# An eight-block transformer kernel, one core: another hand-held order of work for the opening

## The chip, the cores and the metric

The kernel runs on one core of a Trainium2 chip. The metric is the device time of one execution in microseconds; the median of three runs stands for the kernel. Matrix products run on TensorE (PE), reductions and elementwise work on VectorE (DVE), activations and copies on ScalarE (ACT), more elementwise work on GpSimd (POOL), and the loads and stores of the main loop are issued by SyncE (SP).

## The reference

One block of a diffusion transformer with adaptive layer norm, for 8 batches of 512 tokens with 256 features, 16 heads of 16, and a feed-forward part of 2 shared and 16 routed experts of width 128, of which 4 are chosen:

```python
mod = (_silu(L0_c) @ L0_wmod).reshape(L0_c.shape[0], 6, 1, -1)
...
h = _layernorm(x, axis=-1) * (1 + ca) + sa
x = x + ga * _L0_attn_ref(h, ...)
h = _layernorm(x, axis=-1) * (1 + cb) + sb
x = x + gb * _L0_ffn_ref(h, ...)
```

Attention is a softmax of q k^T / 4 per head. The feed-forward part adds gelu(x up) down for the shared experts and the same times a gate for the routed ones; the gate is the softmax of the router, kept for the four largest.

## The kernel before, in words

All float32 products are made of float16 halves: a value is split into a high part and a low rest, and a product takes three matmuls. The high part and the float32 value are written by ScalarE, the low part by GpSimd from the difference.

The work of a batch is cut into items. An item is a triple: kind, number, batch. `PLAN` is one list of all 2690 items, and each of the five engines walks the same list and emits its own share of each item (an item has no share on some engines). So each engine runs its shares strictly in the list's order, and semaphores join them. Banks of PSUM are given out in rings along the list (`ring`), by which an item also waits for the reader of the bank's last user: three banks for what VectorE reads, three for what ScalarE reads, and one more each, lent by the down products until `("up", 0, 0)`.

Kinds that are spoken of here. `first` (8): the q and k of the first half of batch 0 made straight in the layout of the scores; TensorE, two activations, one GpSimd add. `max` (64 per batch): one 128x512 tile of scores and its row maximum on VectorE. `maxT`: the transpose of a group's 16 maxima, copied to the operand `q_aug`, in batch 0 by ScalarE. A group has 16 `max` and 16 `exp`. `exp` (64): the tile of scores again, transposed, now with the maximum taken off by the matmul, and its exponential on ScalarE. `pv` (16): four heads' products with v, from four exps; `oraw` copies a group's sum. `h1T`, `h2T`, `onT`: transposes with a split; `qk`: projections of q and k, with a split; `qk_out` and `qk_in` store them and load them in the layout of the scores; `no_max` copies a row of that. `up`, `gated`, `act_hi`, `down`: the experts; `up` is evicted by ScalarE with Gelu, another table than Exp. `late` 0 and 1: the modulations that are not needed at the start, plain float32 matmuls, read by VectorE. `x_pre` and `x_post`: loads of x. `xg`: residual plus gated bias, on GpSimd.

The expert weights come in eight pieces over three staging places: `stage` n on SyncE loads one (n from 3 on waits for `wlow` n-3), `wsplit` n on ScalarE makes its high part, `wlow` n on GpSimd its low part. `("up", 0, 0)` waits for all eight `wlow`.

`BEGIN` (line 140) is written out by hand: runs of items (kind, batch, first number, last number), 469 items that end in the ninth slot's maxima. `plan` (from the places in the tables above it) appends all other items in the order of their places. A load waits on SyncE for whatever it needs, and everything behind it on SyncE waits with it.

## Time and profile before

| what | us |
|---|---|
| median of three runs | 886.01 (885.74 to 889.5) |
| profiled execution | 884.7 |
| its span, first to last instruction | 882.9 |
| TensorE busy | 832.7 (94%) |
| ScalarE busy | 684.3 (78%) |
| VectorE busy | 605.4 (69%) |
| GpSimd busy | 397.1 (45%) |

A share of busy time is a mean over the whole span. The slices of the page show how it is spread: the opening (some 170 us) has most of the idle time that TensorE has. Matmuls are pipelined and their recorded spans overlap (0.38 us each, a new one each 0.22 us), so a busy TensorE isn't always at its peak. In the chain of waits that ended last, TensorE holds 72%, ScalarE 12%, VectorE 7%.

### The profile page before, as it was taken

How to read it: one execution, taken by the hardware profiler on the slowest of the kernel's cores; microseconds unless marked ns; L12 is line 12 of the kernel's file. 1: busy time of each engine (PE TensorE's matmuls, PEld its weight loads, DVE VectorE, ACT ScalarE, POOL GpSimd, SP SyncE). 2: the span in 40 equal slices, each digit the busy share in tenths (PEclk: the TensorE clock that was granted, in tenths of full speed). 3: DMA queues.
4: the chain of work that ended last, by engine and by line, in shares of the span. 5: the costliest groups of instructions: out<-in, count | busy, mean ns of one | idle time of the engine just before them, and what ended most of it. 6: DMA issues, size and time to landing. Idle time of an engine off the chain costs nothing.

```text
span 882.9 us, 19434 instructions
## 1 busy us (share of the span) xinstructions
PE 832.7 (94%) x7652; PEld 451.1 (51%) x7652; DVE 605.4 (69%) x1207; ACT 684.3 (78%) x1162; POOL 397.1 (45%) x351
## 2 busy tenths in 40 slices
PE   5778788999999999999999999999999999998998
PEld 3222333355545665566555555566555554555555
DVE  5665676786588866977688767886797758632452
ACT  4778688878988889888987899878987787855452
POOL 4455325225643364426623473426533353346472
PEclk9979799999999999999999999999999999999999
DMA  8006300533024512423024401530423300330140
GB/s 260 31 30 159 124 27 13 167 78 118 25 68 157 113 38 65 160 86 90 25 81 156 138 14 61 172 105 2 120 105 78 120 2 2 133 121 1 65 160 25
DMA packets 47306, 77.18 MB, mean 87 GB/s; under 512 B 6408, under 2 KB 41448, under 8 KB 43120
## 3 DMA queue, kind: packets, MB, share of 16 engines
q1 hardware_dynamic: 47216, 75.94, 27.3%
q8 instruction: 61, 1.00, 0.5%
q14 instruction: 29, 0.24, 0.1%
HBM read 63.47 MB, written 12.34 MB: 86 GB/s over the span
## 4 chain that ended last, share of the span: by engine, by line
PE 72%; ACT 12%; DVE 7%; issue 4%; POOL 4%; DMA 1%; SPq 0%; ACTq 0%; DVEq 0%
PE scalar_bank L1028 20%; PE down_bank L1193 18%; PE vector_bank L1101 8%; PE scalar_bank L1084 6%; PE vector_bank L1084 6%; PE vector_bank L1028 5%; ACT probs L787 3%; DVE neg_max L983 3%; PE scalar_bank L1113 3%; ACT q_aug L776 2%; PE vector_bank L1125 2%; ACT rows L759 1%; DVE gelu L970 1%; PE scalar_bank L1137 1%; ACT f_ring L742 1%
## 5 line engine op out<-in xcount | busy, mean ns | idle before, releaser
L983 DVE TENSOR_REDUCE neg_max<-vector_bank 128x1 f16<-128x512 f32 x487 | 309.2, 686 | 93.1 <-PE vector_bank L1084 88.2
L787 ACT ACTIVATE probs<-scalar_bank 128x512 f32<-128x512 f32 x484 | 262.5, 604 | 59.7 <-PE scalar_bank L1084 52.6
L720 POOL TENSOR_TENSOR act_lo<-gelu,act_hi 128x512 f16<-128x512 f32 x144 | 172.8, 1219 | 174.4 <-ACT act_hi L767 153.5
L1193 PE MATMUL down_bank<-down_hi,act_hi 64*128 64x256 f16 x1120 | 175.6, 271 | 0.5 <-PE down_bank L1193 0.2
L1193 PE MATMUL down_bank<-down_hi,act_lo 64*128 64x256 f16 x1120 | 174.6, 270 | 0.0
L1193 PE MATMUL down_bank<-down_lo,act_hi 64*128 64x256 f16 x1120 | 174.5, 269 | 0.0
L1084 PE MATMUL vector_bank<-k_aug,q_aug 64*128 64x512 f16 x487 | 131.1, 385 | 14.7 <-ACT q_aug L776 5.4
L970 DVE TENSOR_TENSOR gelu<-gelu,gates 128x512 f32<-128x512 f32 x128 | 110.1, 881 | 49.5 <-ACT gelu L824 49.4
L1084 PE MATMUL scalar_bank<-q_aug,k_aug 64*128 64x512 f16 x484 | 126.3, 384 | 4.1 <-ACT probs L787 1.9
L824 ACT ACTIVATE gelu<-scalar_bank 128x512 f32<-128x512 f32 x144 | 85.1, 596 | 57.2 <-PE scalar_bank L1028 38.6
L1101 PE MATMUL vector_bank<-probs,v_aug 128*32 128x512 f32 x960 | 111.9, 597 | 1.5 <-DVE z_lo L909 1.5
L1028 PE MATMUL scalar_bank<-z_hi,up_hi 128*128 128x512 f16 x288 | 109.7, 381 | 0.0
L1028 PE MATMUL scalar_bank<-z_lo,up_hi 128*128 128x512 f16 x288 | 109.2, 379 | 0.0
L1028 PE MATMUL scalar_bank<-z_hi,up_lo 128*128 128x512 f16 x288 | 109.2, 379 | 0.0
L767 ACT ACTIVATE act_hi<-gelu 128x512 f16<-128x512 f32 x128 | 76.8, 625 | 25.2 <-DVE gelu L970 19.0
L1193 PEld LDWEIGHTS down_bank<-down_hi,act_hi 64*128 64x128 f16 x1120 | 70.4, 94 | 47.4 <-issue 36.0
L1193 PEld LDWEIGHTS down_bank<-down_lo,act_hi 64*128 64x128 f16 x1120 | 74.8, 94 | 8.6 <-issue 0.2
L1193 PEld LDWEIGHTS down_bank<-down_hi,act_lo 64*128 64x128 f16 x1120 | 74.8, 94 | 5.1
L1084 PEld LDWEIGHTS vector_bank<-k_aug,q_aug 64*128 64x128 f16 x487 | 36.2, 94 | 60.0 <-DVE neg_max L983 22.3
L657 POOL TENSOR_TENSOR z_lo<-f_ring,z_hi 128x512 f16<-128x512 f32 x32 | 36.7, 1158 | 53.8 <-ACT f_ring L742 53.8
L1084 PEld LDWEIGHTS scalar_bank<-q_aug,k_aug 64*128 64x128 f16 x484 | 37.7, 94 | 45.3 <-ACT probs L787 19.9
L1101 PEld LDWEIGHTS vector_bank<-probs,v_aug 128*32 128x32 f32 x960 | 26.8, 109 | 61.9 <-issue 55.4
(202 smaller groups left out, 1258.1 us busy)
## 6 DMA issues: line engine op xcount, KB each, us to landing
gates<-gates_by_expert SPq DMA_DIRECT2D x32, 1024.0 KB, 5.1
q_aug<-q_parts SPq DMA_DIRECT2D x90, 64.0 KB, 2.8
k_aug<-k_parts SPq DMA_DIRECT2D x90, 64.0 KB, 2.6
x_pre<-in_x SPq DMA_DIRECT2D x8, 512.0 KB, 4.8
x_post<-in_x SPq DMA_DIRECT2D x8, 512.0 KB, 6.2
out<-x_post SPq DMA_DIRECT2D x16, 256.0 KB, 4.1
gates<-in_w_up SPq DMA_DIRECT2D x4, 576.0 KB, 10.7
gates<-in_w_down SPq DMA_DIRECT2D x4, 576.0 KB, 5.1
```

The source lines that it names most:

```text
L657: pool.tensor_tensor(lo, f_ring[:, F_RING[kind, n, b][0], :], hi, ALU.subtract).then_inc(s_lo, 1)
L720: pool.tensor_tensor(act[1][:, c, :], gelu[:, n % NGELU, :], act[0][:, c, :], ALU.subtract).then_inc(s_elo, 1)
L767: scalar.activation(act[0][:, act_slot(b, n), :], gelu[:, n % NGELU, :], ACT.Copy).then_inc(s_ehi, 1)
L787: scalar.activation(probs[:, n % U, :], src[:], ACT.Exp, scale=SCALE).then_inc(taken[kind], 1)
L824: scalar.activation(gelu[:, n % NGELU, :], src[:], ACT.Gelu).then_inc(taken[kind], 1)
L970: dve.tensor_tensor(g, g, gates[:, (n - NSH) % 8, :], ALU.mult).then_inc(s_gated, 1)
L983: dve.tensor_reduce(neg_max[:, (u // 2) % TT, at:at + 1], src[:], AX.X, ALU.max, negate=True).then_inc(done, 1)
L1028: ins = pe.matmul(dst, a, b, start=n == 0, stop=n == len(terms) - 1)
L1084: pe.matmul(dst[:], st[at:at + 64, pair, t * P:(t + 1) * P], mo[at:at + 64, pair, :], start=True, stop=True).then_inc(sig, 1)
L1101: ins = pe.matmul(o, v_aug[b % 2][:, kc, h * VW:h * VW + 32], probs[:, u, :], start=kc == 0, stop=kc == TT - 1)
L1113: ins = pe.transpose(dst[:, t * P:(t + 1) * P], a[:, t, n * P:(n + 1) * P], ident[:])
L1193: ins = pe.matmul(o, act[a][at:at + 64, act_slot(b, c), tok:tok + P], wd[w][at:at + 64, c, :], start=n == 0 and k == 0, stop=c == NEX - 1 ...
```

## The change

`BEGIN` is replaced by another list of the same 469 items. The items behind it stay as they are and in the same order; no function changes. The differences on each engine:

- ScalarE: `wsplit` 0 goes from behind `first` 1 to ahead of it, `wsplit` 1 from behind `maxT` 0 to ahead of `first` 5, `wsplit` 5 from behind `exp` 35 to behind `exp` 38 and `qk` 3 of batch 1, `wsplit` 6 and 7 to either side of `exp` 49 of batch 0. One exp is put between `up` 2 and `up` 3.
- TensorE: `late` 0 and `late` 1 are no longer neighbours; seven exps, seven maxima and two `pv` come between them.
- GpSimd: `fill` 0 goes ahead of `first` 7, `wlow` 2 and `fill` 2 ahead of `qk` 1 of batch 1, `wlow` 3 behind `qk` 3, `wlow` 6, `xg` and `wlow` 7 to between `stats1` and `h1T` 0 of batch 2.
- SyncE: `x_post` 0 goes ahead of `stage` 5, `no_max` ahead of the first `qk_in` of batch 1, `qk_in` 2 and 3 of batch 1 ahead of `mods`; behind `qk_in` 0 of batch 2 come `qk_in` 1, `gates_out`, `no_max`; `gates_in` 1 goes behind the `x_pre` of batch 3.
- VectorE: `stats1` and `gm` change place against a few maxima, and the router's steps against a few maxima and an `oraw`.

```diff
-BEGIN = [("x_pre", 1, 0, 0), ("h1T", 0, 0, 1), ("first", 0, 0, 1), ("wsplit", 0, 0, 0), ("qk_out", 0, 2, 2), ("first",
-    0, 2, 2), ("qk_in", 0, 2, 2), ("max", 0, 0, 0), ("first", 0, 3, 3), ("max", 0, 1, 4), ("first", 0, 4, 4), ("max",
-    0, 5, 5), ("qk_out", 0, 3, 3), ("max", 0, 6, 9), ("first", 0, 5, 5), ("qk_in", 0, 3, 3), ("max", 0, 10, 11),
-    ("qk", 0, 2, 2), ("max", 0, 12, 15), ("first", 0, 6, 6), ("maxT", 0, 0, 0), ("wsplit", 0, 1, 1), ("qk", 0, 3, 3),
-    ("stats1", 1, 0, 0), ("gm", 0, 0, 0), ("max", 0, 16, 18), ("exp", 0, 0, 0), ("first", 0, 7, 7), ("exp", 0, 1, 1),
...
-    1), ("max", 0, 32, 32), ("exp", 0, 10, 10), ("max", 0, 33, 34), ("wsplit", 0, 2, 2), ("max", 0, 35, 35), ("stage",
-    0, 3, 3), ("max", 0, 36, 37), ("exp", 0, 11, 13), ("max", 0, 38, 38), ("fill", 0, 2, 2), ("qk", 1, 0, 0), ("max",
-    0, 39, 39), ("pv", 0, 0, 0), ("max", 0, 40, 40), ("exp", 0, 14, 14), ("wlow", 0, 0, 0), ("exp", 0, 15, 15),
-    ("max", 0, 41, 41), ("wlow", 0, 1, 1), ("exp", 0, 16, 16), ("max", 0, 42, 42), ("exp", 0, 17, 18), ("max", 0, 43,
-    43), ("exp", 0, 19, 19), ("pv", 0, 1, 2), ("exp", 0, 20, 20), ("max", 0, 44, 44), ("exp", 0, 21, 21), ("pv", 0, 3,
-    3), ("exp", 0, 22, 22), ("stage", 0, 4, 4), ("exp", 0, 23, 23), ("oraw", 0, 0, 0), ("qk_in", 1, 0, 0), ("max", 0,
-    45, 45), ("exp", 0, 24, 24), ("qk", 1, 1, 1), ("wsplit", 0, 3, 3), ("max", 0, 46, 47), ("maxT", 0, 2, 2),
-    ("no_max", 1, 0, 0), ("exp", 0, 25, 25), ("wlow", 0, 2, 2), ("max", 0, 48, 50), ("exp", 0, 26, 26), ("qk", 1, 2,
...
-    0, 4, 4), ("max", 0, 54, 54), ("exp", 0, 30, 30), ("max", 0, 55, 55), ("qk_out", 1, 1, 1), ("pv", 0, 4, 4),
-    ("max", 0, 56, 58), ("exp", 0, 31, 32), ("pv", 0, 5, 5), ("exp", 0, 33, 34), ("qk_out", 1, 2, 2), ("wlow", 0, 3,
-    3), ("max", 0, 59, 59), ("exp", 0, 35, 35), ("wsplit", 0, 5, 5), ("pv", 0, 6, 6), ("qk", 1, 3, 3), ("pv", 0, 7,
-    7), ("oraw", 0, 1, 1), ("exp", 0, 36, 38), ("max", 0, 60, 61), ("stage", 0, 5, 5), ("exp", 0, 39, 39), ("max", 0,
-    62, 63), ("maxT", 0, 3, 3), ("max", 1, 0, 0), ("qk_in", 1, 1, 1), ("max", 1, 1, 2), ("exp", 0, 40, 40), ("wlow",
-    0, 4, 4), ("wsplit", 0, 6, 6), ("exp", 0, 41, 42), ("max", 1, 3, 5), ("exp", 0, 43, 44), ("late", 0, 0, 0),
-    ("wlow", 0, 5, 5), ("stage", 0, 6, 6), ("late", 0, 1, 1), ("max", 1, 6, 6), ("qk_out", 1, 3, 3), ("x_post", 0, 0,
-    0), ("max", 1, 7, 7), ("exp", 0, 45, 45), ("max", 1, 8, 8), ("stage", 0, 7, 7), ("pv", 0, 8, 9), ("exp", 0, 46,
-    49), ("x_pre", 2, 0, 0), ("max", 1, 9, 11), ("exp", 0, 50, 51), ("max", 1, 12, 12), ("exp", 0, 52, 52), ("pv", 0,
-    10, 11), ("exp", 0, 53, 54), ("mods", 0, 0, 0), ("max", 1, 13, 13), ("exp", 0, 55, 55), ("oraw", 0, 2, 2), ("max",
-    1, 14, 14), ("exp", 0, 56, 56), ("max", 1, 15, 15), ("v", 1, 0, 0), ("maxT", 1, 0, 0), ("max", 1, 16, 16),
-    ("wsplit", 0, 7, 7), ("max", 1, 17, 17), ("exp", 0, 57, 57), ("max", 1, 18, 19), ("ga", 0, 0, 0), ("max", 1, 20,
...
-    0, 1, 1), ("exp", 1, 43, 45), ("max", 1, 59, 61), ("exp", 1, 46, 46), ("max", 1, 62, 62), ("up", 0, 0, 0), ("max",
-    1, 63, 63), ("up", 0, 1, 2), ("maxT", 1, 3, 3), ("max", 2, 0, 1), ("down", 0, 0, 0), ("up", 0, 3, 4), ("exp", 1,
-    47, 48), ("gated", 0, 2, 2), ("pv", 1, 8, 8), ("gated", 0, 3, 3), ("pv", 1, 9, 11), ("act_hi", 0, 1, 3), ("exp",
-    1, 49, 49), ("gated", 0, 4, 4), ("oraw", 1, 2, 2), ("down", 0, 1, 1), ("max", 2, 2, 2), ("act_hi", 0, 4, 4),
...
+BEGIN = [("h1T", 0, 0, 1), ("first", 0, 0, 0), ("wsplit", 0, 0, 0), ("x_pre", 1, 0, 0), ("first", 0, 1, 2), ("max", 0,
+    0, 1), ("first", 0, 3, 3), ("max", 0, 2, 5), ("first", 0, 4, 4), ("wsplit", 0, 1, 1), ("max", 0, 6, 7), ("qk_out",
+    0, 2, 2), ("max", 0, 8, 8), ("qk_in", 0, 2, 2), ("max", 0, 9, 9), ("first", 0, 5, 5), ("max", 0, 10, 11), ("qk",
+    0, 2, 2), ("max", 0, 12, 14), ("first", 0, 6, 6), ("max", 0, 15, 15), ("maxT", 0, 0, 0), ("stats1", 1, 0, 0),
+    ("qk_out", 0, 3, 3), ("qk", 0, 3, 3), ("fill", 0, 0, 0), ("max", 0, 16, 17), ("gm", 0, 0, 0), ("exp", 0, 0, 0),
...
+    ("h1T", 1, 0, 1), ("exp", 0, 5, 5), ("max", 0, 24, 24), ("fill", 0, 1, 1), ("max", 0, 25, 26), ("exp", 0, 6, 7),
+    ("max", 0, 27, 29), ("exp", 0, 8, 9), ("max", 0, 30, 31), ("maxT", 0, 1, 1), ("exp", 0, 10, 10), ("max", 0, 32,
+    36), ("qk_in", 0, 3, 3), ("exp", 0, 11, 11), ("qk_out", 1, 0, 0), ("wsplit", 0, 2, 2), ("max", 0, 37, 37), ("qk",
...
+    ("max", 0, 43, 43), ("exp", 0, 19, 19), ("pv", 0, 1, 1), ("stage", 0, 4, 4), ("pv", 0, 2, 2), ("exp", 0, 20, 20),
+    ("wlow", 0, 0, 0), ("exp", 0, 21, 21), ("max", 0, 44, 44), ("no_max", 1, 0, 0), ("wlow", 0, 1, 1), ("exp", 0, 22,
+    22), ("pv", 0, 3, 3), ("exp", 0, 23, 23), ("oraw", 0, 0, 0), ("wlow", 0, 2, 2), ("exp", 0, 24, 24), ("max", 0, 45,
+    45), ("exp", 0, 25, 25), ("max", 0, 46, 47), ("fill", 0, 2, 2), ("qk", 1, 1, 1), ("maxT", 0, 2, 2), ("wsplit", 0,
...
+    0, 27, 27), ("qk", 1, 2, 2), ("max", 0, 51, 54), ("exp", 0, 28, 30), ("max", 0, 55, 55), ("pv", 0, 4, 4), ("exp",
+    0, 31, 31), ("qk_out", 1, 1, 1), ("max", 0, 56, 56), ("qk_out", 1, 2, 2), ("max", 0, 57, 57), ("x_post", 0, 0, 0),
+    ("stage", 0, 5, 5), ("exp", 0, 32, 32), ("max", 0, 58, 58), ("pv", 0, 5, 5), ("wsplit", 0, 4, 4), ("exp", 0, 33,
+    33), ("max", 0, 59, 59), ("exp", 0, 34, 34), ("pv", 0, 6, 7), ("exp", 0, 35, 38), ("qk", 1, 3, 3), ("max", 0, 60,
+    60), ("wsplit", 0, 5, 5), ("exp", 0, 39, 39), ("oraw", 0, 1, 1), ("max", 0, 61, 63), ("maxT", 0, 3, 3), ("exp", 0,
+    40, 40), ("max", 1, 0, 0), ("exp", 0, 41, 41), ("max", 1, 1, 3), ("qk_in", 1, 1, 1), ("exp", 0, 42, 42), ("max",
+    1, 4, 4), ("exp", 0, 43, 43), ("stage", 0, 6, 6), ("max", 1, 5, 5), ("late", 0, 0, 0), ("exp", 0, 44, 44),
+    ("qk_out", 1, 3, 3), ("max", 1, 6, 8), ("exp", 0, 45, 46), ("pv", 0, 8, 8), ("exp", 0, 47, 47), ("max", 1, 9, 9),
+    ("exp", 0, 48, 48), ("pv", 0, 9, 9), ("wsplit", 0, 6, 6), ("max", 1, 10, 10), ("exp", 0, 49, 49), ("wlow", 0, 3,
+    3), ("wsplit", 0, 7, 7), ("exp", 0, 50, 50), ("max", 1, 11, 12), ("late", 0, 1, 1), ("exp", 0, 51, 52), ("pv", 0,
+    10, 10), ("max", 1, 13, 13), ("pv", 0, 11, 11), ("exp", 0, 53, 53), ("oraw", 0, 2, 2), ("stage", 0, 7, 7), ("max",
...
+    24, 25), ("stats1", 2, 0, 0), ("exp", 0, 62, 63), ("qk_in", 1, 3, 3), ("v", 1, 1, 1), ("mods", 0, 0, 0), ("exp",
+    1, 0, 1), ("pv", 0, 12, 13), ("exp", 1, 2, 3), ("max", 1, 26, 26), ("x_pre", 2, 0, 0), ("rows1", 2, 0, 0), ("exp",
+    1, 4, 4), ("max", 1, 27, 27), ("wlow", 0, 6, 6), ("pv", 0, 14, 14), ("exp", 1, 5, 5), ("pv", 0, 15, 15), ("xg", 0,
+    0, 0), ("wlow", 0, 7, 7), ("exp", 1, 6, 6), ("max", 1, 28, 30), ("oraw", 0, 3, 3), ("ga", 0, 0, 0), ("h1T", 2, 0,
+    0), ("oT", 0, 0, 0), ("exp", 1, 7, 7), ("max", 1, 31, 31), ("oT", 0, 1, 2), ("maxT", 1, 1, 1), ("exp", 1, 8, 8),
+    ("oT", 0, 3, 3), ("max", 1, 32, 33), ("onT", 0, 0, 0), ("exp", 1, 9, 9), ("max", 1, 34, 36), ("onT", 0, 1, 1),
...
+    0, 0, 0), ("max", 1, 62, 63), ("up", 0, 0, 1), ("qk_out", 2, 2, 2), ("gated", 0, 1, 1), ("maxT", 1, 3, 3), ("up",
+    0, 2, 2), ("exp", 1, 47, 47), ("down", 0, 0, 0), ("max", 2, 0, 1), ("up", 0, 3, 4), ("pv", 1, 8, 8), ("gated", 0,
+    2, 3), ("qk_in", 2, 2, 2), ("act_hi", 0, 1, 1), ("gated", 0, 4, 4), ("down", 0, 1, 1), ("exp", 1, 48, 48), ("max",
+    2, 2, 2), ("pv", 1, 9, 11), ("act_hi", 0, 2, 3), ("exp", 1, 49, 49), ("down", 0, 2, 2), ("oraw", 1, 2, 2),
...
+    5), ("v", 2, 0, 0), ("gated", 0, 5, 5), ("down", 0, 18, 19), ("v", 2, 1, 1), ("gates_in", 0, 1, 1)]
```

## Rows read from the trace of the kernel before

**Rows 1.** The page: granted TensorE clock and busy tenths in 40 slices.
```profile
PE   5778788999999999999999999999999999998998
...
PEclk9979799999999999999999999999999999999999
```

**Rows 2.** Busy time by stretch: PE, PEld, DVE, ACT, POOL; then clock, DMA share, GB/s.
```profile
43.00:98.00 55.00, 42.65 (x237) 14.64 (x237) 33.72 (x55) 47.01 (x83) 31.03 (x22) 0.85 0.42 117
...
171.00:197.00 26.00, 25.75 (x242) 14.67 (x242) 19.73 (x41) 19.94 (x33) 6.93 (x7) 1.00 0.39 108
...
240.00:860.00 620.00, 612.53 (x6037) 346.31 (x6033) 439.08 (x868) 494.97 (x839) 284.04 (x248) 1.00 0.27 87
```

**Rows 3.** Timeline of ScalarE, 32 to 43 us: start, duration, line, idle before and releaser.
```profile
32.42 0.78 ACT L799 ACTIVATE act_hi<-scalar_bank,probs 128x512 f16<-128x512 f32 x1 [2.05 <-PE scalar_bank L1137]
...
40.92 1.16 ACT L763 ACTIVATE up_hi<-gates 128x1152 f16<-128x1152 f32 x1
42.11 0.69 ACT L740 ACTIVATE qk_hi<-scalar_bank,bqk 128x512 f16<-128x512 f32 x1
```

**Rows 4.** Timeline of VectorE, 26 to 37 us: first and last of four runs.
```profile
26.35 2.49 DVE L983 TENSOR_REDUCE neg_max<-vector_bank 128x1 f16<-128x512 f32 x4 [1.03 <-PE vector_bank L1084]
...
34.46 2.49 DVE L983 TENSOR_REDUCE neg_max<-vector_bank 128x1 f16<-128x512 f32 x4 [0.43 <-PE vector_bank L1084]
```

**Rows 5.** Timeline of ScalarE, 87 to 108 us: its three longest idle times there.
```profile
87.44 1.16 ACT L763 ACTIVATE down_hi<-gates 128x1152 f16<-128x1152 f32 x1 [1.90 <-DMA gates<-in_w_down]
...
103.33 0.60 ACT L787 ACTIVATE probs<-scalar_bank 128x512 f32<-128x512 f32 x1 [5.10 <-PE scalar_bank L1084]
107.11 0.60 ACT L787 ACTIVATE probs<-scalar_bank 128x512 f32<-128x512 f32 x1 [3.19 <-PE down_bank L1084]
```

**Rows 6.** Timeline of SyncE's issues, 82 to 92 us.
```profile
82.74 2.79 SPq L588 DMA_DIRECT2D k_aug<-k_parts  x6
...
91.93 0.45 SPq L623 DMA_DIRECT2D x_post<-in_x  x1
```

**Rows 7.** DMA view of 82.2 to 86 us: all packets; issues with median time to landing.
```profile
DMA packets 583, 0.98 MB, mean 258 GB/s; under 512 B 70, under 2 KB 456, under 8 KB 583
...
k_aug<-k_parts SPq DMA_DIRECT2D x6, 64.0 KB, 4.3
```

**Rows 8.** Timeline of TensorE, 89 to 105 us: waits, and ends of the late modulations.
```profile
89.81 0.39 PE L1084 MATMUL down_bank<-q_aug,k_aug 64*128 64x512 f16 x1 [1.63 <-ACT f_ring L742]
...
92.03 0.61 PE L1084 MATMUL down_bank<-k_aug,q_aug 64*128 64x512 f16 x1
...
96.06 0.59 PE L1039 MATMUL vector_bank<-chosen,x_post 128*128 128x8 f32 x2
...
102.09 0.67 PE L1044 MATMUL vector_bank<-rows,chosen 128*8 128x256 f32 x2
...
104.83 1.92 PE L1101 MATMUL vector_bank<-probs,v_aug 128*32 128x512 f32 x16 [1.54 <-DVE z_lo L909]
```

**Rows 9.** Busy time by stretch, columns of rows 2: the two at the lower clock.
```profile
54.40:64.70 10.30, 7.83 (x26) 2.10 (x30) 6.30 (x11) 7.52 (x13) 4.07 (x3) 0.50 0.00 0
...
92.00:102.30 10.30, 9.54 (x36) 5.22 (x35) 4.03 (x8) 6.15 (x11) 6.02 (x3) 0.50 0.56 184
```

**Rows 10.** Timeline of ScalarE, 177 to 182 us: last two Gelu items and the switch.
```profile
177.70 0.60 ACT L824 ACTIVATE gelu<-scalar_bank 128x512 f32<-128x512 f32 x1 [1.73 <-PE scalar_bank L1028]
179.00 0.60 ACT L824 ACTIVATE gelu<-scalar_bank 128x512 f32<-128x512 f32 x1 [0.70 <-PE scalar_bank L1028]
179.61 1.28 ACT L787 ACT_TABLE_LOAD   x1
180.90 1.09 ACT L787 ACTIVATE probs<-scalar_bank 128x512 f32<-128x512 f32 x2
```

**Rows 11.** Timeline of GpSimd, 65 to 75 us.
```profile
65.90 4.72 POOL L667 TENSOR_TENSOR up_lo<-gates,up_hi 128x1152 f16<-128x1152 f32 x2
74.44 1.16 POOL L657 TENSOR_TENSOR qk_lo<-f_ring,qk_hi 128x512 f16<-128x512 f32 x1 [3.83 <-ACT f_ring L742]
```

61 lines of the change are left out of this document (28 added, 33 removed).

## The prediction

> **What bounds the kernel now.** I read the page's slices first: TensorE is busy 5 to 8 tenths in the first eight slices and 9 in nearly all that follow, and its granted clock falls twice early on [rows 1]. The table of stretches then says where a list that ends near 197 us can matter: TensorE stands idle 12.35 us of 43 to 98 and 0.25 us of 171 to 197, while from 240 to 860 it idles 7.5 of 620 us [rows 2]. So the opening is bound by waits between engines, the rest by TensorE. Behind the list nothing is reordered: what TensorE gains or loses by the list's end should arrive at the end of the kernel almost whole. ScalarE is the busiest of the others in 43 to 98, 47.01 of 55 us [rows 2]; there a microsecond of its queue is nearly a microsecond of the kernel. The timelines of ScalarE, VectorE, SyncE, TensorE and GpSimd in the opening are then read beside the two lists.
>
> **What the change can be worth.** The two lists hold the same 469 items; I compared each engine's order. No arithmetic is added. Two ScalarE table loads are added, see below. The places that carry the sum:
>
> (a) *The first two weight splits.* `wsplit 0` goes ahead of the second `first`, `wsplit 1` goes from behind the first `maxT` to between `first` 4 and 5. In the trace `wsplit 1` takes 1.16 us at 40.92, right ahead of the `qk` eviction at 42.11 and of the first exps [rows 3]. In its new place ScalarE has stood idle 2.05 us before `first 5` [rows 3], which hides the 1.16 us if the weights are there; if they aren't, the wait stands in front of `first 5` instead. Against the change, `wsplit 0` delays the second `first`, on which the first maximum waits, by the same 1.16 us. VectorE's stream of the first 16 maxima has four gaps after its start, of 1.03, 0.41, 0.41 and 0.43 us [rows 4], 2.28 us in all, which take that up. Bounds: 0 (if VectorE, not ScalarE, ends the stage) to 1.9 us of gain. I take 1.2, because the ScalarE queue behind row 42.11 is unbroken.
>
> (b) *The sixth split and the load ahead of it.* ScalarE waits 1.90 us for a landing before `wsplit 5` at 87.44 [rows 5]. The new list puts `exp` 36 to 38 and the fourth `qk` eviction ahead: three times at most 0.60 us [rows 5] and two activations of 0.69 [rows 3], 3.2 us of work. But it also puts the load of `x_post` on SyncE's queue ahead of that stage and ahead of the six k loads of `qk_in 1` (batch 1); `x_post` went out 9.2 us later before. One such issue takes 0.45 us [rows 6], and 0.5 MB more in front take 2.0 us at the 258 GB/s of that stretch [rows 7], less where the queue has room. So `wsplit 5` comes 3.2 us later in ScalarE's queue and its data 0.45 to 2.45 us later: of the 1.90 us the wait keeps between 0 and 1.2. By itself the gain is 0.7 to 1.9, I take 1.0, near the low end, because the queue moves 258 GB/s there already.
> What is late next is the first maximum of batch 1. Its operands are the same k loads: issued from 82.74 on, over 2.79 us [rows 6], landing 4.3 us after their issue [rows 7], so the last (issued near 85.1) is there near 89.4; TensorE uses them at 92.03 [rows 8]. Spare: 2.6 us. The same 0.45 to 2.45 us go off that, I take 2.1, while what feeds them (`qk 2`) moves ahead with (a) by 1.2. That lets TensorE come to 92.03 earlier by no more than 2.6 + 1.2 - 2.1 = 1.7 us. So (a) and (b) together count 1.7, not 2.2.
>
> (c) *The late modulations.* Today both blocks run back to back, 96.06 to 102.76 on TensorE, all under the lower clock [rows 8, 9]; ScalarE idles 5.10 and then 3.19 us [rows 5]; and TensorE waits 1.54 us for VectorE's six instructions of the second block [rows 8]. The new list puts seven exps, seven maxima and two `pv` between the blocks. TensorE still spends the 6.7 us; it needn't wait the 1.54 us, since exps now stand behind the second block, and ScalarE's idle time is split where exps already queued in filled banks cover a part of each. Bounds: 0, if the wait only moves, to 5, if ScalarE's 8.3 us were what sets the pace. I take 1.5, TensorE's own visible wait, as row 104.83 is the nearest to the end that counts.
>
> (d) *Two more table loads.* The old list runs five `up` without an exp between, the new one `up` 0 to 2, exp 47, `up` 3 and 4, exp 48. That is two more switches of 1.28 us, 2.57 us. ScalarE idles 1.73 and 0.70 us before `up` 3 and 4 [rows 10], 2.43 in all, and exp 47 comes earlier, so I charge 0.5 (bounds 0.1 and 2.6; without the cover, the whole). TensorE has only 0.25 us of idle time in 171 to 197 [rows 2], so it would feel anything uncovered.
> The trace shows a load of 1.28 us at 179.61, right at the end of the activation that starts 179.00 and lasts 0.60, and the next exp starts at 180.90, 1.29 later [rows 10]: nothing more than the load. The Trainium skill's page ScalarE: Activation LUTs, section What ACT_TABLE_LOAD costs, adds a drain of about 1.38 us to each switch. By it the two would cost 5.3 us and the sum would fall by 2.7 us; the trace does not agree.
>
> (e) *GpSimd and SyncE.* `wlow 2` and the last `fill` now precede the second `qk` low part, and `wlow` 6, `xg` and `wlow` 7 precede the low part of `h1T` 2. Two `wlow` take 4.72 us [rows 11], so three end near 65.9 + 7.1 = 73.0 and the `fill` some 1 us later, where the `qk` low part started at 74.44 [rows 11]: free, barely. Behind it wait SyncE's copy of the masked row and the loads after that, needed at 92.03. Later GpSimd has two splits, 4.72 us, and `xg` in front of the low part of `h1T` 2, in a stretch where it waited for ScalarE before; the reader of that part, after `h1T 1`, moved back as well. I charge 0.3 (0 to 4.7). The `gates_in 1` load goes behind four others, and its first reader comes after the list: nothing (if it were late, `gated 6` would wait, right behind the list). Small shifts of a maximum against an exp elsewhere: 0, plus or minus 2, as the single waits in these rows are 0.4 to 2 us.
>
> Sum: 1.7 + 1.5 - 0.5 - 0.3 = 2.4 us. On the profiled execution, 884.7 us (span 882.9 and 1.8 outside), that gives 882.3. The median of the three runs is 886.0, 1.3 above the profiled one, so the prediction is 883.6.
>
> **Rivals.**
> *1, the clock stays up where it falls today (880.2).* From 92.0 to 102.3 the granted clock is 0.50, that is 1.2 instead of 2.4 GHz; TensorE is busy 9.54 of 10.3 us there. From 54.4 to 64.7 it is the same with 7.83 us [rows 9]. Not long ahead of the second fall TensorE had stood idle 1.63 us [rows 8], behind (b)'s wait. If the new order fills this hole, the two late blocks take 3.4 instead of 6.7 us, and the sum becomes 2.4 + 3.4 = 5.8. For it: the hole lies just where list and wait are changed. Against: the new `wsplit 5` may still wait, and the first fall, near 54, lies where little is changed.
> The Trainium skill's page TensorE: Matmul & The Clock Gate, section HAM oscillation, says idle gaps bring the clock down and re-warming is paid each time, which is this mechanism; it does not say which way this list turns it.
> *2, the gain is given back to landings and maxima (885.7).* The k loads come 2.45 us later, the maxima bound the opening, and the late blocks' wait moves to the next `pv`. Then 1.7 and 1.5 shrink to 0.7 and 0.4, less 0.8: 0.3. This is also the case in which the list doesn't do what its recorded landings promise: once order changes, landings change with it. For: spare at 92.03 is only 2.6 us.
> *3, slower: one more stretch at the lower clock (888.4).* A stretch costs up to half of TensorE's busy time in it, 9.54/2 = 4.8 us [rows 9]. It decides where a hole like that before 92.0 opens in otherwise dense work: the fresh table loads, which hold up exps at 176 to 181, or a second fall near 115. 886.0 - 2.4 + 4.8 = 888.4; on top of rival 2 890.5.
>
> **How the numbers follow.** Forecast 0.45 (2.4 us, its bounds 0.5 to 4.4: 881.6 to 885.5); rival 1 0.22; rival 2 0.18; rival 3 0.15. The range leaves a tenth on each side: the low end is rival 1's, 880.2, the high end reaches over rival 3's middle, 889.0. Half a per cent is 4.4 us, about what a measurement tells from no change here. Faster by more: most of rival 1 and a tail of the forecast, 0.24. Slower by more: rival 3 with rival 2, 0.07. The same: 0.69.
>
> **What would show it.** (a): `wsplit 1` right behind `first 4`, and the `qk` eviction of 42.11 near 40.9. (b): wait before `wsplit 5` under 1.9 us, first maximum of batch 1 at 90.3 or later instead of 92.03, perhaps with a wait for a k landing. (c): no ScalarE gap over 3 us between 98 and 108. (d): two more table loads between 170 and 200, idle time before `up` 3 and 4 gone, exp 48 within 1 us of its place relative to `up 0`. (e): no TensorE wait on GpSimd near 134. I am wrong if TensorE's idle time in 0 to 171 falls by over 5 us, or grows; or if the number of clock falls changes, which moves the time by more than my whole sum.

## The result, and the profile after

The changed kernel takes 891.84 us (890.87 to 892.90); the kernel before, beside it, 885.88 (884.78 to 889.50). The ratio is 1.0055, with a 95% interval of 1.0034 to 1.0077: slower by 6.0 us, where 2.4 us faster was forecast and 889.0 was the upper end of the range. The kernel before spreads widely: of its 31 runs beside the first experiments ten took 888.1 to 892.1 us at a granted clock of 0.974 to 0.978, the others 884.1 to 886.9 at 0.980 to 0.986. The profiled execution took 892.9 us with a span of 891.1; of the kernel before it is 884.7 and 882.9.

From the page of after, busy tenths of TensorE and its granted clock in 40 slices of 22.3 us, against [rows 1]:

```profile
PE   5877869899999999999999999999999999998998
PEclk9989688999999999999999999999999999999999
```

The clock row has a 6 in the fifth slice where it was a 7, and two 8s behind it where all was at 9. The stretches, columns as in [rows 2], say how much:

```profile
43.00:98.00 55.00, 41.41 (x236) 14.47 (x233) 33.72 (x56) 44.98 (x79) 26.70 (x17) 0.87 0.40 114
119.20:132.30 13.10, 8.24 (x57) 2.85 (x56) 11.49 (x20) 5.10 (x10) 9.07 (x6) 0.89 0.00 1
131.40:138.30 6.90, 6.05 (x24) 3.96 (x24) 5.26 (x12) 2.21 (x4) 1.19 (x2) 0.51 0.00 0
171.00:197.00 26.00, 24.43 (x177) 9.84 (x176) 19.50 (x33) 23.02 (x39) 5.70 (x5) 1.00 0.46 149
240.00:860.00 620.00, 612.61 (x6038) 346.06 (x6031) 439.81 (x872) 498.94 (x846) 287.01 (x252) 1.00 0.27 87
```

From 240 to 860 TensorE is idle as much as before (7.4 of 620 us against 7.5), so nothing was lost behind the reordered part. In 119.2 to 132.3 it works 8.24 of 13.1 us, and right behind that the granted clock is 0.51, the lower level of 1.2 GHz, for 6.9 us. (The stretch of 171 to 197 holds other items now, `up 0` having moved from 170.9 to 177.9, so its columns aren't compared.) I compared when TensorE starts the same item in the two traces; the difference, after minus before, runs down the list like this:

```text
item            start after   after - before
h1T 0, batch 1      48.4        -0.9
maxT 2              72.2        -2.4
maxT 3              91.0        -0.7
v 1, batch 1       119.2        -0.9
h1T 0, batch 2     132.8        +5.8
maxT 1, batch 1    137.4        +6.9
up 0               177.9        +7.1
up 5               201.0        +8.3
down, batch 7      886.3        +8.2
```

Up to 119 us the new list led, by 2.4 us at its best. It then lost 6.7 us between two items that lie 13.6 us apart, another 1.1 under the lower clock, 0.2 up to `up 0`, and 1.2 around the `up` items. From `up 5` on the difference doesn't move: what is won or lost by the list's end does arrive whole at the kernel's end, as forecast, here with the other sign.

*The loss at 125.* The timeline of VectorE of after, 123 to 133 us (start, duration, line, idle time before and its releaser), then its four `rows` instructions by their source line (shortest, median, longest in ns):

```profile
124.36 0.69 DVE L983 TENSOR_REDUCE neg_max<-vector_bank 128x1 f16<-128x512 f32 x1 [1.60 <-PE vector_bank L1084]
124.97 6.61 DVE L841 TENSOR_SCALAR rows<-x_pre,mean_var,rstd 128x256 f32<-128x256 f32 x4
...
L841 DVE TENSOR_SCALAR rows<-x_pre,mean_var,rstd x4: 819/1766/2499, 125.0 to 129.1; 128x256 f32<-128x256 f32 x4
```

Over the whole kernel before, the same view of that line reads:

```profile
L841 DVE TENSOR_SCALAR rows<-x_pre,mean_var,rstd x28: 404/407/413, 11.5 to 589.5; 128x256 f32<-128x256 f32 x28
```

Four instructions of 0.41 us have taken 6.61 us together, and no wait for another engine is shown for them. What GpSimd did meanwhile (timeline of GpSimd of after), and what TensorE then waited for (timeline of TensorE of after):

```profile
123.53 2.38 POOL L667 TENSOR_TENSOR down_lo<-gates,down_hi 128x1152 f16<-128x1152 f32 x1
125.87 0.78 POOL L672 TENSOR_TENSOR hit<-ga_all,bo_all 128x256 f32<-128x256 f32 x1
126.73 2.34 POOL L675 TENSOR_TENSOR x_post<-x_post,hit 128x1024 f32<-128x1024 f32 x1
129.03 2.41 POOL L667 TENSOR_TENSOR down_lo<-gates,down_hi 128x1152 f16<-128x1152 f32 x1
...
132.25 0.61 PE L1084 MATMUL vector_bank<-k_aug,q_aug 64*128 64x512 f16 x1 [4.86 <-DVE neg_max L983]
```

Laid side by side, the `rows` instructions end at 126.06, 126.80, 129.22 and 131.59; GpSimd's end at 125.91, 126.65, 129.07 and 131.44. Each `rows` instruction ends 0.15 us behind one of GpSimd. The first and the last GpSimd row are the two splits, the two between them are `xg`. In the kernel before, those steps were elsewhere: `xg` at 132.57, the two splits at 96.36 and 117.71.

### The profile page after: what moved, and what is told of

It is laid out like the page before. It is cut to its first block, busy times and chain, and to the rows that moved or that the text cites. A ratio compares the mean times of both kernels' runs of the same rounds, so it can differ in the third digit from the quotient of the medians.

```text
span 891.1 us, 19436 instructions
## 1 busy us (share of the span) xinstructions
PE 839.9 (94%) x7652; PEld 452.5 (51%) x7652; DVE 610.3 (68%) x1207; ACT 687.5 (77%) x1164; POOL 396.9 (45%) x351
## 4 chain that ended last, share of the span: by engine, by line
PE 81%; DVE 8%; ACT 5%; issue 2%; POOL 2%; DMA 1%; SPq 0%; ACTq 0%; DVEq 0%; POOLq 0%
PE scalar_bank L1028 23%; PE down_bank L1193 19%; PE vector_bank L1101 10%; PE vector_bank L1084 7%; PE scalar_bank L1084 7%; PE vector_bank L1028 5%; DVE neg_max L983 3%; PE scalar_bank L1113 3%; PE vector_bank L1125 2%; PE scalar_bank L1137 1%; ACT probs L787 1%; DVE gelu L970 1%; ACT q_aug L776 1%; DVE rows L841 1%; PE vector_bank L1090 1%
## 5 line engine op out<-in xcount | busy, mean ns | idle before, releaser
L720 POOL TENSOR_TENSOR act_lo<-gelu,act_hi 128x512 f16<-128x512 f32 x144 | 172.9, 1219 | 175.8 <-ACT act_hi L767 154.4
L970 DVE TENSOR_TENSOR gelu<-gelu,gates 128x512 f32<-128x512 f32 x128 | 109.6, 876 | 49.9 <-ACT gelu L824 49.0
L1028 PE MATMUL scalar_bank<-z_hi,up_hi 128*128 128x512 f16 x288 | 109.6, 381 | 0.0
L1193 PEld LDWEIGHTS down_bank<-down_hi,act_hi 64*128 64x128 f16 x1120 | 70.4, 94 | 49.3 <-issue 37.2
L1084 PEld LDWEIGHTS scalar_bank<-q_aug,k_aug 64*128 64x128 f16 x485 | 37.3, 94 | 48.0 <-ACT probs L787 20.5
## 6 DMA issues: line engine op xcount, KB each, us to landing
gates<-in_w_up SPq DMA_DIRECT2D x4, 576.0 KB, 10.4
```

The lines of the kernel that those rows point to most:

```text
L720: pool.tensor_tensor(act[1][:, c, :], gelu[:, n % NGELU, :], act[0][:, c, :], ALU.subtract).then_inc(s_elo, 1)
L970: dve.tensor_tensor(g, g, gates[:, (n - NSH) % 8, :], ALU.mult).then_inc(s_gated, 1)
L1028: ins = pe.matmul(dst, a, b, start=n == 0, stop=n == len(terms) - 1)
L1084: pe.matmul(dst[:], st[at:at + 64, pair, t * P:(t + 1) * P], mo[at:at + 64, pair, :], start=True, stop=True).then_inc(sig, 1)
L1193: ins = pe.matmul(o, act[a][at:at + 64, act_slot(b, c), tok:tok + P], wd[w][at:at + 64, c, :], start=n == 0 and k == 0, stop=c == NEX - 1 ...
```

## The theory and its rival, and how they were told apart

Theory: VectorE's SBUF-to-SBUF `TENSOR_SCALAR` can't finish while a GpSimd instruction runs. Step (e) put four GpSimd instructions back to back onto the four of `rows`, maxima stood behind them in VectorE's queue, TensorE waited for a maximum, and its clock fell. Rival: the loss is of the forecast's own kind (landings and maxima come late, or an extra clock fall by a hole elsewhere, rivals 2 and 3), and the long `rows` only fill time that was idle anyway.

Every experiment but `e4_rows_by_scalar` moves whole items in the list; `plan` gets this loop, and the diffs below show only the dict:

```diff
+    for item, ahead in MOVES.items():
+        begin.remove(item)
+        begin.insert(begin.index(ahead) + 1, item)
```

### The GpSimd steps taken away, put in, and one alone

`e1_pool_away`, from the kernel after:

```diff
+    ('wlow', 6, 0): ('wlow', 5, 0),
+    ('wlow', 7, 0): ('wlow', 6, 0),
+    ('xg', 0, 0): ('h1T', 0, 2),
```

> The changed list, with GpSimd's two last weight splits ahead of the statistics of batch 2 and the residual with bias behind the first low part of batch 2, so that nothing of GpSimd runs beside VectorE's four rows instructions of batch 2. Theory (VectorE's four instructions are held by GpSimd's): they take 1.4 us together again instead of 6.6, TensorE's idle time of 4.9 us before the maximum 30 of batch 1 goes, with it the lower clock behind it, and the kernel comes to 885 to 886.5, 0.994 of the changed one. Rival (the loss lies in the order of the other engines, the holding is hidden): 890 to 892.

Measured: 885.41 us (884.17 to 886.24), ratio to before 0.9986 (0.9967 to 1.0004), 6.4 us less than after. VectorE's timeline of this kernel in the same place:

```profile
124.33 1.37 DVE L849 TENSOR_SCALAR rows<-x_pre,mean_var,rstd 128x256 f32<-128x256 f32 x4
```

The wait of 4.86 us and the lower clock from 131.4 to 138.3 are gone with it. In the profiles TensorE has won 7.4 us on after by `maxT 1` of batch 1. Of these, 0.9 are there at `v 1` already, ahead of the collision. From `v 1` to `maxT 1` it takes 11.8 us (busy 11.5) where after takes 18.3 (busy 13.4): 4.5 us of idle time less, and 1.9 us of busy time less for the same matmuls, which in after ran at the lower clock in part.

`e2_pool_on_rows`, from the kernel before, puts in (e)'s collision and nothing else:

```diff
+    ('wlow', 6, 0): ('stats1', 0, 2),
+    ('xg', 0, 0): ('wlow', 6, 0),
+    ('wlow', 7, 0): ('xg', 0, 0),
```

> The kernel before, with one thing of the new list: split 7, the residual with bias and split 8 on GpSimd between the statistics and the first low part of batch 2, beside VectorE's rows. Theory: the four instructions take 6 to 7 us together, and the kernel is 5 to 7.5 us slower than before, 891 to 893.5. Rival (not these but the rest of the list): within 1 us of before.

Measured: 892.35 us (890.43 to 893.18), ratio 1.0056 (1.0038 to 1.0075). VectorE's timeline:

```profile
129.00 6.32 DVE L849 TENSOR_SCALAR rows<-x_pre,mean_var,rstd 128x256 f32<-128x256 f32 x4
```

Of the whole change, this one part alone makes the kernel before as slow as after. Its single profile is not all collision: TensorE is 3.3 us behind the kernel before at `v 1` of batch 1 already, with lower clock also from 41.4 to 44.8 and up to 109.6 instead of 102.2, where the edit does no more than take one GpSimd split away (96.36 in the kernel before). The collision's own stretch, from `v 1` to `maxT 1`, takes 15.9 instead of 10.4 us. The medians rest on ten and more runs, and fastest against fastest it is 890.43 against 884.14. Again the four end 0.15 us behind a GpSimd instruction each: at 129.79, 130.53, 132.96 and 135.33, where GpSimd's end at 129.63, 130.38, 132.81 and 135.18.

`e3_one_split_on_rows`, from the kernel before, puts one split there:

```diff
+    ('wlow', 7, 0): ('stats1', 0, 2),
```

> The kernel before with only the eighth split (2.4 us of GpSimd) moved behind the statistics of batch 2. Theory (held until GpSimd's instruction ends): the first of the four rows instructions lasts from 124.5 to GpSimd's end near 126.6, 2.1 us, the other three 0.41 each; the kernel is 1 to 2.5 us slower than before, 887 to 888.5. Rival (the two engines share the rate): all that overlap are stretched alike, by less than two, and none much above 0.8 us.

The timelines of GpSimd and VectorE of this kernel, and the four by source line:

```profile
125.99 2.38 POOL L673 TENSOR_TENSOR down_lo<-gates,down_hi 128x1152 f16<-128x1152 f32 x1
...
126.33 3.16 DVE L847 TENSOR_SCALAR rows<-x_pre,mean_var,rstd 128x256 f32<-128x256 f32 x4
...
L847 DVE TENSOR_SCALAR rows<-x_pre,mean_var,rstd x4: 402/403/2189, 126.3 to 129.1; 128x256 f32<-128x256 f32 x4
```

The first lasted from 126.33 to 128.52, 0.15 us behind the split's end, and the other three took 0.40 each. With a shared rate, more than one would be stretched and GpSimd's split would be longer than 2.38 us. It isn't: one waits out the other. The time was 885.8 us (ratio 0.9991, 0.9966 to 1.0016), where 887 to 888.5 was expected: the 1.8 us that VectorE loses here don't show in it. In the traces TensorE takes 7.8 us from `v 1` to `h1T` 0 of batch 2 instead of 6.9 in the kernel before, but 51.1 instead of 50.8 to `up 0`. So 0.9 us of the hold came through, and all but 0.3 was made up behind it.

### The same GpSimd work, the rows on ScalarE

`e4_rows_by_scalar`, from the kernel after, gives the four instructions of batch 2 to ScalarE and leaves GpSimd's splits and `xg` where they were, with two small GpSimd instructions (0.24 and 0.20 us) ahead of them:

```diff
-                    if b == 1:
+                    if b in (1, 2):
...
-                        pool.wait_ge(s_bias1, 1)
-                        pool.wait_ge(s_rs1, 4)
+                        pool.wait_ge(s_bias1, 2 * b - 1)
+                        pool.wait_ge(s_rs1, 2 * b + 2)
...
-                elif kind == "rows1" and b == 1:
-                    scalar.wait_ge(s_bias1, 2)
+                elif kind == "rows1" and b in (1, 2):
+                    scalar.wait_ge(s_bias1, 2 * b)
...
-                elif kind == "rows1" and b > 1:
+                elif kind == "rows1" and b > 2:
```

> The changed kernel with its list as it is; only the rows of batch 2 are made by ScalarE (as those of batch 1 are), four activations of 0.6 us and two small GpSimd instructions more, so GpSimd's splits and the residual stay where they are but VectorE does nothing beside them that is held. Theory (only VectorE's instruction of this kind and GpSimd exclude each other): the activations take 0.6 us each as ever, the hole of 4.9 us is down to about 1, and the kernel comes to 886 to 888. Rival (whatever reads or writes there is slowed by GpSimd): the activations are stretched too, and the time stays at 890 or more.

Measured: 886.27 us, ratio 0.9995 (0.9977 to 1.0014). The timelines of ScalarE and GpSimd:

```profile
124.92 2.06 ACT L759 ACTIVATE rows<-x_pre,mean_var,rstd 128x256 f32<-128x256 f32 x4
...
125.85 2.36 POOL L680 TENSOR_TENSOR x_post<-x_post,hit 128x1024 f32<-128x1024 f32 x1
```

Four activations of 0.59 to 0.60 us, started 0.49 apart, go through beside the very GpSimd instructions that held VectorE, and the longest wait of TensorE there is 1.1 us. So it isn't the tiles or the memory as such, it is VectorE against GpSimd; and taking away either side of the collision returns 5.6 to 6.4 us. The rival is out.

### The forecast's other steps, one at a time

All of these but `e9_first_splits_only` contain the edit of `e1_pool_away`, and are read against its 885.41 us. The medians of the kernel before beside the experiments lie within 0.4 us (886.10, 886.17, 886.53), so a few tenths between two experiments mean nothing.

`e9_first_splits_only`, from the kernel before, is step (a) alone:

```diff
+    ('wsplit', 0, 0): ('first', 0, 0),
+    ('wsplit', 1, 0): ('first', 4, 0),
```

> The kernel before with only the first two weight splits moved as in the change: the first ahead of the second projection of the opening, the second behind the fifth. My forecast: ScalarE's qk eviction and the first exps 1.2 us earlier, and as much off the kernel, 884.9. Rival (VectorE's maxima end the opening, and other orders of the new list made the 0.9 us by which it led at the transposes of batch 1): no change, 886, and those transposes within 0.4 us of before.

Measured: 886.32 us, ratio 1.0003 (0.9976 to 1.0029). ScalarE's timeline of this kernel, then of `e3_one_split_on_rows`, which has the opening of the kernel before and in its profile, as this one, the lower clock from 42.5 to 46.0:

```profile
42.95 0.60 ACT L794 ACTIVATE probs<-scalar_bank 128x512 f32<-128x512 f32 x1
44.97 0.78 ACT L806 ACTIVATE act_hi<-scalar_bank,probs 128x512 f16<-128x512 f32 x1 [1.42 <-PE scalar_bank L1144]
```

```profile
44.12 0.60 ACT L793 ACTIVATE probs<-scalar_bank 128x512 f32<-128x512 f32 x1
44.96 0.78 ACT L805 ACTIVATE act_hi<-scalar_bank,probs 128x512 f16<-128x512 f32 x1 [0.24 <-PE scalar_bank L1143]
```

The first exp comes 1.17 us earlier, and ScalarE then stands idle 1.42 instead of 0.24 us for TensorE's eighth `first`, whose eviction starts where it did (44.97 and 44.96); TensorE comes to `maxT 1` of batch 0 at 57.42 and 57.41. So in this pair (a) by itself gains nothing. Two limits: the interval of the ratio is about 2.3 us to either side and doesn't rule out the forecast 1.2, and in both profiles the eighth `first` ran at the lower clock, in the kernel before's own profile it didn't. There its eviction stands at 43.74, right behind the first exp with no idle time. What (a) gains in that case is not shown.

`e6_sixth_split_later` mends (b): the load and the split go back behind what they were put ahead of.

```diff
+    ('x_post', 0, 0): ('qk_out', 3, 1),
+    ('wsplit', 5, 0): ('oraw', 1, 0),
```

> The mended list, with the load of x_post of batch 0 back behind the k store of batch 1 and the sixth weight split behind the copy of the second group's sum. Theory (the split that waits for its landing held up that copy, and the copy the bank for the third transpose of maxima): TensorE's wait of 3.4 us before that transpose falls under 1.5 us, and late 0 starts 1.5 to 2.5 us earlier; the time falls by 0.5 to 2 us against the first experiment, if nothing behind takes it back. Rival (maxima or a k landing end that wait anyway): the wait stays above 2.5 us.

Measured: 883.54 us, ratio 0.9967 (0.9951 to 0.9984). What was wrong with (b) is in the timelines of ScalarE, TensorE and SyncE of the kernel after:

```profile
88.83 1.16 ACT L763 ACTIVATE down_hi<-gates 128x1152 f16<-128x1152 f32 x1 [1.44 <-DMA gates<-in_w_down]
91.02 0.61 PE L1090 MATMUL vector_bank<-ident,neg_max 128*128 128x128 f16 x4 [3.44 <-ACT o_raw L771]
...
81.23 0.45 SPq L623 DMA_DIRECT2D x_post<-in_x  x1
81.72 0.56 SPq L545 DMA_DIRECT2D gates<-in_w_down  x1
```

ScalarE waits 1.44 us for the weights; behind the split in its queue stand an exp and `oraw 1`, which frees the bank in which TensorE makes `maxT 3`, and TensorE waits 3.44 us for it. The order on ScalarE turned a wait for a load into one of TensorE for a bank. In `e1_pool_away`, from which this experiment starts, the same two waits are 0.5 and 2.5 us. Here TensorE's wait is, in the table of waits:

```profile
PE vector_bank L1100 <- DVE neg_max L993: 1.5, 1, 1.5
```

and the split waits for nothing. `late 0` starts 2.2 us earlier than in after, 0.8 of which the mending adds to `e1_pool_away`. The median falls by 1.9, more than the 1.0 by which that wait got shorter. What else differs in the two profiles is told under the next experiment.

`e7_late_together` undoes (c):

```diff
+    ('late', 1, 0): ('late', 0, 0),
```

> The mended list with the two blocks of late modulations together again. My forecast held them apart to be worth 1.5 us. If so, this is 1 to 2 us slower than the first experiment, 886.4 to 887.4. Rival (apart they leave ScalarE as much idle time as together, in more pieces, since TensorE's own time is what counts): within 0.5 us of it, and TensorE reaches the first v of batch 1 within 0.5 us of the same place.

Measured: 884.25 us, ratio 0.9973 (0.9958 to 0.9988), 1.2 us less than with the blocks apart; the two intervals overlap, but in the traces too `v 1` of batch 1, behind both blocks in either order, starts 1.3 us earlier. The tables of waits of ScalarE, 90 to 112 us (total, times, longest), of this kernel, then of `e1_pool_away`:

```profile
ACT probs L796 <- PE scalar_bank L1093: 6.6, 1, 6.6
ACT probs L796 <- PE down_bank L1093: 1.6, 1, 1.6
ACT q_aug L785 <- PE vector_bank L1099: 0.5, 1, 0.5
```

```profile
ACT probs L795 <- PE scalar_bank L1092: 8.2, 6, 3.5
ACT q_aug L784 <- PE vector_bank L1098: 0.5, 1, 0.5
```

8.7 us of idle time either way, once in a block and once in six pieces. Nothing of it was covered by taking the blocks apart. That explains a gain of 0, not the loss of 1.2, and neither of the two cases expected (1 to 2 us slower, or within 0.5) came. The profiles show another difference: the lower clock lasts from 90.1 to 103.8 in `e1_pool_away` and from 90.1 to 100.4 here. In the 3.4 us between, TensorE is busy 3.4 there, which at half the clock cost up to 1.7. That stretch near 90 lasts 13.6 or 13.7 us in the profiles of after, `e1_pool_away`, `e5_two_loads_less` and `e11_old_tail`, and 10.2 or 10.3 in those with the late blocks together or the sixth split later, or both (`e6_sixth_split_later`, `e8_three_mended`, `e10_all_and_old_tail`, `e12_late_and_sixth` and this one). `e4_rows_by_scalar` is the exception, with 10.3 and a stretch of its own at 78.1. So the shorter stretch goes with either gain; that it makes them is argued from one profile each, not shown.

`e5_two_loads_less` puts exp 47 back behind the fifth `up`, which takes (d)'s two table loads out:

```diff
+    ('exp', 47, 1): ('up', 4, 0),
```

> The mended list of the first experiment (GpSimd's three pieces away from the rows), and exp 47 of batch 1 behind up 4, so that five up run without an exp between and two table loads go. The profile of the changed kernel lost 1.2 us between up 0 and up 5. Theory (the two loads cost what ScalarE's idle time doesn't cover): that loss goes, 0.8 to 1.3 us less than the first experiment, 884.1 to 884.7. Rival (they were covered, the loss is of the order of the down products): no change, and the shift between up 0 and up 5 stays over 0.8 us.

Measured: 885.57 us, ratio 0.9986 (0.9970 to 1.0002), the same as `e1_pool_away`: the two loads cost nothing that the medians show. But 1.2 us do go between `up 0` and `up 5`, with or without them. `e11_old_tail` leaves the new list up to `up 0` and sorts all behind it in the old order (`old` is the list of the kernel before):

```diff
+    at = begin.index(("up", 0, 0))
+    begin[at:] = sorted(begin[at:], key=old.index)
```

> The list of the first experiment with everything from the first up item on in the order of the list before, nothing else. Theory (the order of up, down and pv costs the 1.2 us): the shift between up 0 and up 5 is under 0.3 us, the time 884.0 to 884.6 against 885.4. Rival (state, not order): the shift stays over 0.8 us and the time at 885.4.

Measured: 882.49 us (881.26 to 884.05), ratio 0.9948 (0.9925 to 0.9970). The stretch from `up 0` to `up 5`, TensorE's busy time, of this kernel and then of `e1_pool_away`:

```profile
169.00:191.00 22.00, 21.44 (x209) 1.00 0.44 152
```

```profile
170.30:193.50 23.20, 22.41 (x209) 1.00 0.44 145
```

209 matmuls either way take 22.0 instead of 23.2 us. The start differences to before agree: -1.84 at both ends here, -0.54 and then +0.66 there. So the tail's own part in the profiles is 1.2 us. The median fell by 2.9, where 0.8 to 1.4 was expected. Of the rest the profiles show 1.3 us that this kernel leads by at `up 0` already, with the same list up to there, and 1.6 us far behind it: the profile of `e1_pool_away` has one more stretch at the lower clock, from 748.9 to 752.3 us, and this one hasn't. Across it the lead on after, which has such a stretch too, stays at 7.6 us there and grows from 10.1 to 11.7 here, 1.6 us.

### Put together

`e8_three_mended` is `e6_sixth_split_later` with exp 47 behind the fifth `up`; `e12_late_and_sixth` is it with `late 1` behind `late 0`; `e10_all_and_old_tail` is the latter with the old order behind `up 0`.

> The mended list with both the table loads and the sixth split mended. If the two gains add, 2 to 3 us under the first experiment and under the kernel before, 882.5 to 884. If what is gained before the third transpose is given back in the maxima behind, only the loads' part remains, 884.1 to 884.7.

> The first experiment's list with the late blocks together and the sixth split and x_post later, the tail as in the change. If the two gains (1.2 and 1.9 us of the medians) add: 882.0 to 882.8. If they are the same gain taken twice, because both act through how long TensorE stands idle near 90 and so through the lower clock there: 883.3 to 884.3.

> The changed list with GpSimd's three pieces away from the rows, the late blocks together, the sixth split and x_post later, and everything from the first up item on in the order of the list before. If the old order of the up, down and pv items is worth the 1.2 us that every version of the new list lost between up 0 and up 5: that loss goes to under 0.3 us and the time is 881 to 883. If the loss goes with the state in which the stretch is entered and not with its order: it stays over 0.8 us, and the time is 882.5 to 884.5.

| kernel | us | ratio to before (95%) |
|---|---|---|
| `e8_three_mended` | 883.96 | 0.9976 (0.9964 to 0.9987) |
| `e12_late_and_sixth` | 883.10 | 0.9956 (0.9935 to 0.9976) |
| `e10_all_and_old_tail` | 881.49 (880.58 to 882.28) | 0.9947 (0.9931 to 0.9962) |

`e8_three_mended` agrees that the loads are free (nothing on top of 883.54). In `e12_late_and_sixth` the gains of 1.9 and 1.2 us come to 2.3 together. That lies between the two cases expected; adding up (3.1) isn't ruled out by an interval of 1.8 us to either side, and its stretch at the lower clock is no shorter than with one of them (10.2 us). From it to `e10_all_and_old_tail` the old tail is worth 1.6 us. `e10_all_and_old_tail` beats both kernels: 5.0 us less than the 886.53 of the kernel before beside it, 10.4 less than after. Its stretch of the `up` items, columns as in [rows 2]:

```profile
171.00:197.00 26.00, 25.44 (x250) 14.84 (x249) 19.27 (x41) 18.83 (x32) 6.92 (x7) 1.00 0.36 122
```

## Why the prediction was wrong, step by step

**(e) is the step that failed.** The edit and its place were seen: two splits and `xg` "in front of the low part of `h1T` 2, in a stretch where it waited for ScalarE before". It was costed as a queue: who waits behind GpSimd's work, with bounds of 0 to 4.7 us and a price of 0.3. Nobody waited; the sign named for it (no wait of TensorE for GpSimd near 134) came out right and said nothing. The cost ran across engines without a semaphore: 6.61 instead of 1.38 us on VectorE, 5.2 us more, a hole of 4.86 us on TensorE, and a clock fall behind the hole. By `e1_pool_away` the step is worth 6.4 us, by `e2_pool_on_rows` 6.3, over the 886.10 beside it.

It could have been read in the kernel before. Its timelines of VectorE and GpSimd in the first microseconds:

```profile
2.78 4.20 DVE L846 TENSOR_SCALAR probs<-probs 128x16 f32<-128x16 f32 x1 [2.78 <-ACT probs L726]
...
2.40 1.80 POOL L642 MEMSET q_aug<- 128x2048 uint32 x1
4.15 1.80 POOL L643 MEMSET k_aug<- 128x2048 uint32 x1
5.90 1.06 POOL L644 MEMSET v_aug<- 128x1152 f32 x1
```

Sixteen elements a partition in 4.20 us, ended at 6.98, where the last fill ends at 6.96. That the fills caused it is argued from the ends alone; no run moved them, and it is not quite the later pattern, as VectorE didn't get through between two fills. The stronger sign in the kernel before is in the gating by VectorE, two inputs in SBUF:

```profile
L970 DVE TENSOR_TENSOR gelu<-gelu,gates x128: 656/692/1639, 178.6 to 870.1; 128x512 f32<-128x512 f32 x128
```

Of the 128, 38 take 0.94 us or more; every one of them starts while a GpSimd instruction of 128x512 runs and ends 0.54 to 0.55 us behind that one's end. Had I asked which instruction runs far over the usual time of its form, and what the other engine does meanwhile, these rows would have given the price: a VectorE instruction of such a form lasts until the GpSimd one beside it has ended. The Trainium skill has a rule on it: the page SBUF — State Buffer, section Who interferes with whom, says that VectorE and GpSimd share a port pair, that whoever issues first gets it for the whole instruction while the other blocks, and that `tensor_scalar` is among the forms that can ask for it, if its operands meet conditions. The traces agree on the holding (2189 ns against 402 in `e3_one_split_on_rows`); that it goes through the ports no run here can show. The rule spoke against this change, and the prediction didn't weigh it.

**(a), forecast 1.2.** The sign came right, the `qk` eviction moved from 42.11 to 40.40, and no gain of its own was seen: 0 in the pair of `e9_first_splits_only`, where it is lost at the eighth `first`. The argument was that ScalarE's queue is unbroken behind row 42.11 [rows 3]. It was so in the kernel before's profile. In that of `e3_one_split_on_rows`, with the lower clock there, the eighth `first` comes from TensorE later and has its eviction 2.0 us behind that of `qk` (42.96 and 44.96). So the queue is unbroken only while TensorE keeps ahead of it, which the sum left out. The new list does lead in the opening: it comes to `h1T` 0 of batch 1 at 48.3 to 48.5 in all its profiles, the old one at 49.3, 50.4 and 50.9. As (a) alone stays at 50.9, its other orders make that lead; which of them was not tried.

**(b), forecast 1.0, capped with (a) to 1.7.** The wait kept 1.44 of 1.90 us, where 0 to 1.2 was allowed. The first maximum of batch 1 comes at 91.96 on TensorE, 0.07 us earlier than before, within what was said (90.3 or later), but out of a lead that had been 2.4 at `maxT 2`; by `maxT 3` the stretch has lost 1.7 us. The cap was looked for in the k landings; it was the bank that `oraw 1` frees. The step named what the landing would delay in SyncE's queue, and left out what stood behind the split in ScalarE's.

**(c), forecast 1.5.** Of the opposite sign: -1.2 by `e7_late_together`. ScalarE has a gap over 3 us after all, in the timeline of after:

```profile
99.65 0.60 ACT L787 ACTIVATE probs<-scalar_bank 128x512 f32<-128x512 f32 x1 [3.51 <-PE scalar_bank L1084]
```

TensorE's visible wait of 1.54 us was taken for the gain. While a block runs, TensorE makes nothing that ScalarE could read, wherever the block stands; so there was nothing to win, and the loss goes with 3.4 us more at the lower clock.

**(d), forecast -0.5.** The two loads came (1.28 us each, exp 184.16 to 184.76, next load at 184.78) and on ScalarE exp 48 stands 8.35 us behind `up 0`, 8.17 before. Their cost doesn't show in the medians (885.57 with two loads less, 885.41 with them), so 0.5 was, if anything, too much. 1.2 us went in the same stretch by the order of the other items, which the step didn't price.

**The rivals.** Rival 3 had the sign and said what decides: a hole like that before 92.0 in otherwise dense work. It was looked for at 115 and at 176; it came at 127. Its price of 4.8 us is the clock's alone. Here the hole itself was most of the loss: against `e1_pool_away`, from `v 1` to `maxT 1`, 4.5 us are idle time and 1.9 the longer busy time under the lower clock. Rival 1's mechanism didn't happen: of the first 150 us, 20.5 were at the lower clock before and 30.8 after (56.3 to 63.2, 90.5 to 104.1, 117.8 to 121.2, 131.4 to 138.3). Of the signs named for being wrong, the number of clock falls came (four in the first 150 us instead of two) and the idle time didn't (37.9 us of the first 171, 38.2 before). The falls and the stretch near 750 move single profiles by 0.8 to 3.3 us with no edit that explains it, as much as or more than the steps (a) to (d) were each worth.

So the sum of 2.4 us held three gains, of which the first didn't show and the others were about -1.7 and -1.2, one cost that was 0 with a neighbour of 1.2, and one of 0.3 that was 6.4.

One premise of the whole sum fails too, that idle time taken from TensorE is time won. Up to `up 0`, `e1_pool_away` has 4.8 us less of it than the kernel before (33.4 and 38.2), and yet is there only 0.5 us earlier, for TensorE is busy 136.9 instead of 132.7 us with as many matmuls. Of these 4.2 us the 3.4 us more at the lower clock account for up to 1.7; the rest is open.

**Left open.** Which orders of the opening give its lead; which of the items behind `up 0` cost the 1.2 us; whether the gains at the sixth split and at the late blocks are one and the same stretch of lower clock; what makes the clock fall at 117 and near 750. None of these was tried by itself.

## What to carry to other kernels

When work moves on GpSimd, lay VectorE's timeline beside its new place and look for elementwise instructions from SBUF to SBUF (here `TENSOR_SCALAR`, and `TENSOR_TENSOR` with both inputs there): each can cost a whole GpSimd instruction, and nothing waits on a semaphore to show it. Look first for instructions far over the usual time of their form, in the kernel before as well; their cause is often in another engine's row. And a recorded landing time is no reason to put a wait in a queue: what counts is what stands behind it, here the release of a bank.
